# Last chunk of an attention-and-FFN kernel: layer-norm statistics split by head, epsilon moved to VectorE, the last tile handled in halves, three output tiles routed over ScalarE and GpSimd

## The reference, cut to what matters

```
x = x + attention(layernorm(x), Wq, Wk, Wv, memory, ...)
m = mean(x); v = var(x); n = (x - m) / sqrt(v + eps)
x_fp8 = clip(n / s, -448, 448).astype(float8_e4m3)
x = x + (x_fp8 * s) @ (weight * weight_scale).T
```

## Time and profile before

| what | value |
|---|---|
| median of 3 runs | 2020.57 us (2020.05 to 2024.47) |
| profiled execution, own time | 2019.41 us |
| span of the profiled execution | 2017.6 us |
| TensorE busy | 2000.8 us (99% of the span) |
| ScalarE busy | 1937.0 us (96%) |
| VectorE busy | 1116.0 us (55%) |
| GpSimd busy | 132.1 us (7%) |
| chain that ended last | PE 93%, DVE 3%, DMA 2%, ACT 1% |

### The profile page before, as it was taken

One profiled execution on the slowest core, in us unless ns is written; L12 is line 12 of the kernel. 1 busy time (PEld: TensorE's weight loads), 2 busy tenths in 40 slices (PEclk: granted clock), 3 DMA queues, 4 the chain that ended last, 5 costly groups with the idle time before them and its releaser, 6 DMA issues.

```text
span 2017.6 us, 63258 instructions
## 1 busy us (share of the span) xinstructions
PE 2000.8 (99%) x27820; PEld 907.9 (45%) x27828; DVE 1116.0 (55%) x1733; ACT 1937.0 (96%) x2191; POOL 132.1 (7%) x164
## 2 busy tenths in 40 slices
PE   8999999999999999999999999999999999999998
PEld 7876533344444444444444444444444444444445
DVE  7786544555455545554555445554555455554555
ACT  5667999999999999999999999999999999999997
POOL 5761000000000000000000000000000000000000
PEclk9999999999999999999999999999999999999999
DMA  6755111121111211121111211121112212221111
GB/s 198 256 198 181 49 49 37 40 52 52 36 41 50 72 46 37 52 72 48 31 48 51 73 38 44 52 73 40 37 49 52 72 31 52 52 72 32 45 50 47
DMA packets 132471, 131.67 MB, mean 65 GB/s; under 512 B 28387, under 2 KB 107643, under 8 KB 132219
## 3 DMA queue, kind: packets, MB, share of 16 engines
q1 hardware_dynamic: 131355, 126.24, 22.3%
q10 hardware_dynamic: 864, 1.57, 0.2%
HBM read 86.57 MB, written 37.49 MB: 61 GB/s over the span
## 4 chain that ended last, share of the span: by engine, by line
PE 93%; DVE 3%; DMA 2%; ACT 1%; issue 1%; POOL 0%; SPq 0%; ACTq 0%; DVEq 0%; POOLq 0%
PE ps L935 43%; PE ps L997 43%; PE ps L821 2%; DMA resid<-in_x 2%; PE ps L1037 1%; PE ps L1021 1%; DVE stats L1164 1%; PE ps L1090 1%; PE ps L1107 1%; DVE ps L1321 0%; DVE y_out L1309 0%; DVE parts L1229 0%; ACT parts L671 0%; PE ps L794 0%; PE ps L775 0%
## 5 line engine op out<-in xcount | busy, mean ns | idle before, releaser
L754 ACT ACTIVATE pool<-ps 128x1024 f32<-128x1024 f32 x1953 | 1795.1, 1164 | 3.7 <-PEq L973 0.8
L935 PE MATMUL ps<-q_st,k_st 99*32 99x512 bf16 x16128 | 1100.5, 378 | 0.7 <-issue 0.4
L997 PE MATMUL ps<-pool,v_st 128*32 128x512 f32 (+1 forms) x8568 | 1061.6, 567 | 0.0
L935 PEld LDWEIGHTS ps<-q_st,k_st 99*32 99x32 bf16 x16128 | 438.2, 95 | 812.5 <-issue 498.2
L997 PEld LDWEIGHTS ps<-pool,v_st 128*32 128x32 f32 x8568 | 270.0, 110 | 210.8 <-issue 0.6
L1450 DVE STREAM_TRANSPOSE by_token<-ps 128x512 f32<-128x512 f32 x63 | 45.2, 717 | 476.6 <-PE ps L997 476.6
L1443 DVE SCALAR_TENSOR_TENSOR late<-late 128x1024 f32<-128x1024 f32 x189 | 231.5, 1225 | 6.5
L1429 DVE TENSOR_SCALAR late<-ps 128x512 f32<-128x512 f32 x126 | 87.1, 691 | 127.2 <-PE ps L935 127.2
L631 POOL TENSOR_TENSOR var_eps<-moments,eps 128x1 f32<-128x1 f32 x32 | 6.1, 190 | 1810.5 <-DVE moments L1479 1810.5
L1506 DVE SCALAR_TENSOR_TENSOR y_out<-ps,scalars,resid 128x512 f32 (+1 forms) x28 | 21.0, 751 | 112.2 <-PE ps L1021 112.2
L1434 DVE SCALAR_TENSOR_TENSOR late<-late 128x1024 f32<-128x1024 f32 x63 | 77.2, 1225 | 2.1
(11 more groups left out here) (150 smaller groups left out, 1001.4 us busy)
## 6 DMA issues: line engine op xcount, KB each, us to landing
v_st<-v_aug SPq DMA_DIRECT2D x64, 256.0 KB
q_aug<-parts SPq DMA_DIRECT2D x32, 384.0 KB, 3.3
q_st<-q_aug SPq DMA_DIRECT2D x64, 192.0 KB
k_st<-k_aug SPq DMA_DIRECT2D x64, 192.0 KB
k_st<-k_aug SPq DMA_DIRECT2D x192, 64.0 KB
sigma_kept<-y_out SPq DMA_DIRECT2D x32, 256.0 KB, 3.7
q_st<-q_aug SPq DMA_DIRECT2D x64, 128.0 KB
wqT<-sigma_kept SPq DMA_DIRECT2D x32, 256.0 KB, 5.2
```

The lines of the kernel that those rows point to most:

```text
L754: act.activation(held[:, half_u * 2 * CH:half_u * 2 * CH + 2 * CH], sc[unit % SLOTS].rearrange("p a b -> p (a b)"), ACT.Exp, scale=EXP_UNIT)\
L935: last = pe.matmul(dst[VW * c:VW * c + VW, :], k_st[0:AUG, par, keys:keys + VW], q_st[0:AUG, par, q * CH:q * CH + CH], start=True, stop=True)
L997: last = pe.matmul(acc[par][VW * c:VW * c + VW, :].rearrange("v (i s) -> v i s", s=VW)[:, places, :], v_st[:, par, j, :], by_place[:, c, p ...
```

## The change

It has five parts. (1) Before the last chunk's tiles, VectorE takes bn_stats of the first seven heads' columns (448 of 512) of all four tiles; when a tile's last head has been added, it takes those of the last 64 columns, and bn_aggr joins the two. (2) For all tiles VectorE adds epsilon, which GpSimd did, and GpSimd only takes the power. `round_to_float8` subtracts the mean in an instruction of its own that doesn't wait for GpSimd, and multiplies by `rstd` and `inv_s` in the next one; the tiny instruction that made `rstd_s` is gone. (3) The last tile's last rounding step, its turn, its copy, its product, its output and its store are in two halves of 256 columns; the second half's copy out of PSUM is VectorE's. (4) The outputs of the last chunk's tiles 0 to 2 are scaled by ScalarE into `y_out`, and GpSimd adds `resid` to them. (5) The filler turns are 8 and not 20.

```diff
@@ pool
             with pool_e.Fori(0, NT) as i:
-                pool_e.wait_ge(f_moments, i + 1)
-                pool_e.tensor_tensor(var_eps[:, 0:1], moments[:, 0, 0:1, 1], eps[:, 0:1], ALU.add).then_inc(f_eps, 1)
                 pool_e.wait_ge(f_eps, i + 1)
                 pool_e.tensor_tensor(rstd[:, 0, 0:1], var_eps[:, 0:1], minus_half[:, 0:1], ALU.pow).then_inc(f_rstd, 1)
                 pool_e.wait_ge(f_rstd, i + 1)
+            for t in range(TPC - 1):
+                pool_e.wait_ge(y_scaled, t + 1)
+                pool_e.tensor_tensor(y_out[:, t, :], y_out[:, t, :], resid[:, NT - TPC + t, :], ALU.add).then_inc(y_ready, 1)
@@ act
             for t in range(TPC):
                 act.wait_ge(xq_turned, t + 1)
-                act.activation(last_xqT[:, t, :, :].rearrange("p k s -> p (k s)"), last_ffn_tp[t % 2], ACT.Copy)\
+                ks = KT if t < TPC - 1 else KT // 2
+                act.activation(last_xqT[:, t, 0:ks, :].rearrange("p k s -> p (k s)"), last_ffn_tp[t % 2][:, 0:ks * P], ACT.Copy)\
                     .then_inc(xqT_ready, 1)
+                if t == 1:
+                    act.wait_ge(y_stored, 16 * NG)
+                for scaled in ((), (0,), (1, 2), ())[t]:
+                    act.wait_ge(ffn_ready, NT - TPC + scaled + 1)
+                    act.activation(y_out[:, scaled, :], last_ffn[scaled], ACT.Copy, scale=sw).then_inc(y_scaled, 1)
@@ dve
+            def gather_moments(i, groups):
+                dve.bn_aggr(moments[:, 0, 0, :], groups).then_inc(f_moments, 1)
+                dve.wait_ge(f_moments, i + 1)
+                dve.tensor_tensor(var_eps[:, 0:1], moments[:, 0, 0, 1:2], eps[:, 0:1], ALU.add).then_inc(f_eps, 1)
+
+            def last_moments_but_one_head(t):
+                dve.bn_stats(last_stats[:, t, 0, :], by_head(t, 0, HEADS - 1))
+
+            def last_moments(t):
+                dve.drain()
+                dve.bn_stats(last_stats[:, t, 1, :], by_head(t, HEADS - 1, 1))
+                dve.drain()
+                gather_moments(NT - TPC + t, last_stats[:, t, :, :].rearrange("p a s -> p (a s)"))
@@ round_to_float8
+                dve.tensor_scalar(xs, row, moments[:, 0, 0, 0:1], None, ALU.subtract).then_inc(f_step, 1)
+                dve.wait_ge(f_step, i * FLOAT8_STEPS + 1)
                 dve.wait_ge(f_rstd, i + 1)
-                dve.tensor_scalar(rstd_s[:, 0:1], rstd[:, 0, 0:1], inv_s, None, ALU.mult).then_inc(f_step, 1)
-                dve.wait_ge(f_step, i * FLOAT8_STEPS + 1)
-                dve.tensor_scalar(xs, row, moments[:, 0, 0, 0:1], rstd_s[:, 0:1], ALU.subtract, ALU.mult).then_inc(f_step, 1)
+                dve.tensor_scalar(xs, xs, rstd[:, 0, 0:1], inv_s, ALU.mult, ALU.mult).then_inc(f_step, 1)
...
@@ the end of the program
-            for t in range(TPC):
-                add_last_tile(t)
-                tile_moments(NT - TPC + t)
-                if t == TPC - 1:
-                    last_out(0)
-                round_to_float8(NT - TPC + t, xq[:, t, :], last_chunk=True)
-            for t in range(1, TPC):
-                last_out(t)
+            dve.drain()
+            for t in range(TPC):
+                last_moments_but_one_head(t)
+            for t in range(TPC):
+                add_last_tile(t)
+                last_moments(t)
+                round_to_float8(NT - TPC + t, xq[:, t, :], last_chunk=True)
+            dve.wait_ge(xq_turned, TPC + 1)
+            dve.tensor_copy(last_xqT[:, TPC - 1, KT // 2:KT, :].rearrange("p k s -> p (k s)"), last_ffn_tp[0][:, 0:HALF])\
+                .then_inc(xqT_half_ready, 1)
+            dve.wait_ge(y_stored, 16 * NG)
+            last_out_by_halves()
```

More of the change, by code:

```diff
@@ L47 @@
 WARM_UP_TURNS = 20
+LAST_TURNS = 8
 LATE = 2
@@ L105 @@
 FLOAT8_STEPS = 6
+HALF = DM // 2
 FFN_PRODUCT_AT = (10, 14, 18, 22)
@@ L169, in attention_ffn @@
         stats = sb("stats", [P, TPC, 6], F32)
+        last_stats = sb("last_stats", [P, TPC, 2, 6], F32)
         moments = sb("moments", [P, 2, TPC, 2], F32)
@@ L246, in attention_ffn @@
         last_ffn = [ps[:, 2 + t, :] for t in range(TPC)]
+        last_ffn_half = [ps[:, i, 0:HALF] for i in (5, 7)]
         x_loaded = [sem(f"x_loaded{i}") for i in range(2)]
@@ L336, in attention_ffn @@
         xq_ready = sem("xq_ready")
+        xq_half_ready = sem("xq_half_ready")
         xq_turned = sem("xq_turned")
+        xqT_half_ready = sem("xqT_half_ready")
         turn_begun = sem("turn_begun")
@@ L342, in attention_ffn @@
         y_ready = sem("y_ready")
+        y_scaled = sem("y_scaled")
+        y_half_ready = sem("y_half_ready")
         y_stored = sem("y_stored")
@@ L542, in _ @@
             store_chunk(NG - 2)
-            for t in range(TPC):
+            for t in range(TPC - 1):
                 sp.wait_ge(y_ready, (NG - 1) * TPC + t + 1 + ONE_FREE)
                 sp.dma_start(out_tiles[:, NT - TPC + t, :], y_out[:, t, :]).then_inc(y_stored, 16)
-            sp.wait_ge(y_stored, 16 * (NG + TPC))
+            for i in range(2):
+                sp.wait_ge(y_half_ready, i + 1)
+                sp.dma_start(out_tiles[:, NT - 1, i * HALF:i * HALF + HALF], y_out[:, TPC - 1, i * HALF:i * HALF + HALF])\
+                    .then_inc(y_stored, 16)
+            sp.wait_ge(y_stored, 16 * (NG + TPC + 1))
         @block.gpsimd
@@ L1145, in _, with half_product @@
             last_ffn_product(TPC - 2)
-            for i in range(WARM_UP_TURNS):
+            for i in range(LAST_TURNS):
                 pe.transpose(last_ffn[TPC - 1][:, 0:P], ident[:, :], ident[:, :])
-            last_ffn_turn(TPC - 1)
-            last_ffn_product(TPC - 1)
+            last_tile = TPC - 1
+            pe.wait_ge(xqT_ready, last_tile)
+            for i in range(2):
+                pe.wait_ge((xq_half_ready, xq_ready)[i], (1, NT)[i])
+                for k in range(KT // 2):
+                    cols = (i * KT // 2 + k) * P
+                    last = pe.transpose(last_ffn_tp[1 - i][:, k * P:k * P + P], xq[:, last_tile, cols:cols + P], ident_bf[:, :])
+                last.then_inc(xq_turned, 1)
+            def half_product(i, ks):
+                for k in ks:
+                    last = pe.matmul(last_ffn_half[i], last_xqT[:, last_tile, k, :], wT_ffn[:, k, i * HALF:i * HALF + HALF],
+                                     start=(k == 0), stop=(k == KT - 1))
+                if KT - 1 in ks:
+                    last.then_inc(ffn_ready, 1)
+            pe.wait_ge(xqT_ready, TPC)
+            for i in range(2):
+                half_product(i, range(KT // 2))
+            pe.wait_ge(xqT_half_ready, 1)
+            for i in range(2):
+                half_product(i, range(KT // 2, KT))
         @block.vector
@@ L1500, in round_to_float8 @@
                     dve.wait_ge(xqT_loaded, i * 16 * KT + SIXTEEN_FREE)
-                dve.tensor_tensor(rounded, xs, big, ALU.subtract).then_inc(xq_ready, 1)
+                if not (last_chunk and i == NT - 1):
+                    dve.tensor_tensor(rounded, xs, big, ALU.subtract).then_inc(xq_ready, 1)
+                else:
+                    dve.tensor_tensor(rounded[:, 0:HALF], xs[:, 0:HALF], big[:, 0:HALF], ALU.subtract).then_inc(xq_half_ready, 1)
+                    dve.tensor_tensor(rounded[:, HALF:DM], xs[:, HALF:DM], big[:, HALF:DM], ALU.subtract).then_inc(xq_ready, 1)
             def ffn_out(g, t):
```

17 lines of the change are left out of this document (10 added, 7 removed).

## The result

The changed kernel took 2023.91 us in the median (2022.35 to 2026.9, 22 runs), the kernel before 2020.58 us on the same chips (22 runs). The ratio is 1.0016, with a 95% interval of 1.0010 to 1.0022, so it is 3.2 us slower (2.0 to 4.4), within the 0.2% that I had called no change.

A forecast was written before the change was run, and what follows sets the result against it. TensorE was taken to bound the kernel up to the last tile, so only the final 9.61 us could change: -1.41 + 2.7 (holds) + 0.4 (power) + 0.7 (clock) = +2.4 us on 2020.57, giving 2023.0, range 2018.9 to 2024.9.

The forecast's parts named there:

- Tile 3 can't begin earlier: Last chunk: tile 3 waits for TensorE's last weighing, whatever VectorE saves on tiles 0 to 2; 0, bounds 0 to +0.1.
- The time of day that I gave as a sign: Sign in the profile: tile 3's transpose at 2005.3 to 2005.5, the span near 2020.
- Statistics: Tile 3's chain: bn_stats of 64 columns at 0.23 in place of 512 at 0.69, -0.46 us.
- Epsilon and the mean: Between bn_aggr and the product: -0.29 us from the new order, +0.4 from GpSimd's power running behind the subtraction.
- Halves: From tile 3's last rounding step to the last output's end: two halves of 256 columns gain 0.66 us.
- The three holds: Tile 3's rounding: each GpSimd sum holds a wide VectorE step, one-input too, by 0.9 us, +2.7; chance 0.50.
- TensorE's clock: Last turns and products: after some 3.5 us of idling TensorE runs at 1.2 GHz, +0.7 us (bounds 0 and 1.0).
- The store: After the last output: landing takes the same 2.0 us (bounds 0 and -0.3).
- only two-input steps are held: Rival, tile 3's rounding: sums hold only VectorE steps with two SBUF inputs, total -0.3 us, 2020.3; chance 0.22.
- no holds: Rival, tile 3's rounding: GpSimd's sums lie wholly beside VectorE, total -1.4 us, 2019.2; chance 0.13.
- VectorE keeps its turn: Rival: GpSimd's sums get in only after VectorE's rounding, near 2011.7, delaying last stores, +0.7 us, 2021.3; chance 0.07.
- Slow f32 sums: Rival: each f32 sum holds VectorE for 2.13 us, +6.1, 2026.7; chance 0.08 together with a loss elsewhere.

The follow-up runs named there:

- e10: The changed kernel run again unchanged, for a second profile: 12.12 us from tile 3's transpose start to the last output's end.
- e9: The kernel before, run again unchanged against itself: ratio 1.0001 (0.9992 to 1.0010).
- e1: The changed kernel without GpSimd's three sums, ScalarE's scalings kept: ratio to the kernel before 0.9999 (0.9990 to 1.0008).
- e6: The changed kernel with GpSimd's three sums waiting for the end of tile 3's rounding: ratio to the kernel before 1.0014 (1.0005 to 1.0024).
- e3: The changed kernel with 38 filler turns and not 8: ratio 1.0014 (1.0005 to 1.0023).
- e4: The kernel before with only outputs 0 to 2 scaled by ScalarE and summed by GpSimd: ratio 1.0017 (1.0007 to 1.0026).
- e5: The changed kernel with each GpSimd sum replaced by a one-input multiplication by 1.0; one profile, no time compared.
- e8: The changed kernel, loop rounding as before, outputs 0 and 1 on VectorE, output 2 by ScalarE and, after tile 3's rounding, GpSimd: ratio 1.0005 (0.9996 to 1.0014).
- e2: The changed kernel with outputs 0 to 2 back on VectorE, without ScalarE's scalings and GpSimd's sums: ratio 0.9999 (0.9990 to 1.0008).

## Why the prediction was right

I had said 2023.0 with a range of 2018.9 to 2024.9 and 0.90 for within 0.2%. It came out at 2023.91, by the ratio +3.2 where I had +2.4. Step by step:

- **Tile 3 can't begin earlier: right.** VectorE idled 0.53 before it, and began 0.07 us after the last weighing's end, as before. The four bn_stats made ahead took 2.21 and cost nothing: from the last whole-head transpose to tile 3's start it is 28.47, before 28.46. The time of day that I gave as a sign, 2005.3 to 2005.5, came out at 2007.23 (2006.55 in e10), and so the span at 2022.1 and not near 2020. That isn't the change's doing as far as the runs show: the kernel before, run again in e9, began tile 3 at 2008.44.
- **Statistics: right.** From the transpose's start to bn_aggr's it is 1.43, before 1.89: -0.46.
- **Epsilon and the mean: the net right in size, the mechanism not as told.** From bn_aggr's start to the first step behind the power it is 1.30, before 1.36. The power beside the subtraction took 0.72 and not 0.54: +0.18, where I had taken +0.4. So the net is -0.06, forecast +0.11. The power didn't run behind the subtraction: it began at 2009.14, 0.16 after the subtraction's start and 0.32 before its end, and was longer. The product began 1.09 after bn_aggr's end, not 1.2 to 1.3.
- **Halves: the gain a little too high.** From that step's start to the last output's end it was 6.36, and is 2015.58 - 2009.76 = 5.82 in e1: -0.54, forecast -0.66. The sum without the sums' holds was -1.41 + 0.4 = -1.01, and e1 measured 8.56 - 9.61 = -1.05. That these agree so well is in part luck, since the halves gave 0.12 less than forecast, and epsilon and the mean 0.17 more.
- **The three holds: right.** Forecast +2.7, measured 3 x 0.94 = +2.82. The step that I had to choose was whether one-input steps are held as well. They were, all three, and the two-input ones weren't met by a sum. I had given this case 0.50, so it was no sure forecast. My reason for it, that a one-input step is fast because it draws on both ways into SBUF, is tested by no run. The size is right in part by luck. I read 0.90 from a VectorE operation of one column beside a bf16 operation of 1.04. An f32 sum takes 1.26 in e6 and 1.44 to 1.55 beside the rounding. "Almost the whole" of such a sum, by the same share of 0.87, would have been 1.1 a hold and 3.3 for three. The measured 0.94 is three quarters of 1.26: the price of the sum was too low and the share too high. And the held steps don't end just before the sums' ends, as I had said, but 0.28 or 0.29 after them.
- **TensorE's clock: right.** Forecast +0.7, e3 gave +0.71.
- **The store: about right.** From the last output's end to the span's end it was 2.64 and 2.45 in the two profiles of the kernel before, and 2.74 and 3.03 in those of the changed kernel.

The tail's terms add up to -1.05 + 2.82 + 0.71 = 2.48 of 2.52. The rest of the 3.2 is 0.1 to 0.6 of the stores' end and what the ratio's interval leaves open. The beginning of the heads (the first whole-head transpose) lay between 207.6 and 210.4 us in thirteen profiles, the same kernel at 207.6 and 210.2, so single executions differ there by more than the change is worth.

Of the rivals, "only two-input steps are held" and "no holds" are refuted by the three rows of 1.37. "VectorE keeps its turn" is refuted by the first sum's end at 2011.64, in the middle of the rounding. "Slow f32 sums" had the right direction, since a sum is longer than I took it to be, but GpSimd's length isn't what VectorE loses: 0.94 of 1.44 to 1.55.

The Trainium skill's rule (SBUF — State Buffer, "SBUF: two separate sides") that a GpSimd operation and a VectorE operation that uses two ports or has two SBUF inputs block each other, and that whichever starts first goes first, agrees with the three rows of 1.37 and with the sums of e4, 1.27 when first and 1.45 when second. That the one-input steps run in a 2-port mode no row shows. The rule's words "for the whole instruction" don't agree: in e5 L1560, with two SBUF inputs, finished its 0.42 of work 0.60 before GpSimd's operation ended, and in e4 L1500 was let in 0.27 before the first sum's end.

## What to carry to other kernels

Moving work to an idle GpSimd is not free for VectorE: three sums of 512 columns beside a chain of wide SBUF steps cost that chain 0.94 us each and 0.71 more through TensorE's clock, where the same outputs on VectorE, put into its waits, cost 0.58 together. If GpSimd must do wide operations, e6 found no hold beside VectorE work that reads PSUM, but there they ended too late for the last stores. Look in the trace for steps of one line that are longer in one place than elsewhere. And a chain that grows makes TensorE idle, so ask what its last matmuls cost at the lower clock. A saving at the very end of a kernel also has to get past its stores: in e8 0.93 us less of computing gave 0.16 to 0.35 us in the profiles, and the ratio showed no gain.

## What the runs showed of the hardware that I had not expected

- The hold isn't set by the length of GpSimd's operation alone: two-input sums of 1.44 to 1.55 us cost VectorE 0.94 per sum, one-input operations of 1.50 to 1.76 cost 0.28 to 0.42 a step. Whether the inputs or the kind of operation makes the difference is open.
- A GpSimd operation is lengthened too: a sum took 1.27 when it began ahead of the VectorE step, 1.44 to 1.55 when a step was already running, and the one-column power 0.54 beside an output that reads PSUM, 0.72 beside the subtraction.
- The granted clock fell to 0.50 while TensorE idled, for 3.61 us in the changed kernel and 3.00 us in e4, and was 1.00 through the products of e2, before which it had idled 1.36 us. In e5, after 2.05 us, the products began at 1.00 and the clock fell while they ran (0.76 in the stretch from 2015, 0.50 from 2016), so they took 1.35 between 1.05 and 1.89.
